# A segment softmax that divides by a second exponential, shares read from PSUM, node rows loaded in an earlier stage, and record scatters moved between stages

## The reference

```python
q, k, v = (x @ W + b).reshape(n, H, C)            # H = 4 heads, C = 32, for each of q, k, v
e  = (edge_attr @ We).reshape(-1, H, C)
kj, vj = k[src] + e, v[src] + e
alpha = einsum('ehc,ehc->eh', q[dst], kj) / sqrt(C)
amax  = segment_max(alpha, dst)
ex    = exp(alpha - amax[dst])
denom = segment_sum(ex, dst)
alpha = ex / (denom[dst] + 1e-16)                 # a softmax over the edges of one destination
agg   = segment_sum(vj * alpha[:, :, None], dst)
out   = agg.reshape(n, HID) + (x @ Wskip + bskip)  # then a two-layer gelu MLP on out
```

## Time and profile before

| what | us |
|---|---|
| median of 3 runs | 5401.89 (5398.77 to 5412.19) |
| span of the profiled execution | 4651.0 |
| softmax stage | 2062 to 2195 |
| weighing stage | 2197 to 2399 |
| stage of m1 and l2 | 2401 to 2568 |

### The profile page before, as it was taken

One profiled execution on the slowest core, in us unless ns is written; L12 is line 12 of the kernel. 1 busy time (PEld: TensorE's weight loads), 2 busy tenths in 40 slices (PEclk: granted clock), 3 DMA queues, 4 the chain that ended last, 5 costly groups with the idle time before them and its releaser, 6 DMA issues. The chain is left out here.

```text
span 4651.0 us, 50018 instructions
## 1 busy us (share of the span) xinstructions
PE 2871.3 (62%) x13750; PEld 2210.0 (48%) x13751; DVE 2230.8 (48%) x2711; ACT 613.9 (13%) x1076; POOL 3414.1 (73%) x3213
## 2 busy tenths in 40 slices
PE   3799998967777777751989643444444333333333
PEld 1688887943333333331989433333333333333333
DVE  7899997656666666668971621111111111111112
ACT  0355554010000000001751000000000000000000
POOL 1888886857777777767867677777777777777775
PEclk8899999968877878875999866666666566555556
DMA  6466566816666666651989523222222122212221
GB/s 191 139 189 183 170 187 209 265 37 172 170 170 170 170 171 173 173 153 59 278 241 276 174 68 94 68 68 68 68 68 68 49 53 52 53 53 53 53 53 51
DMA packets 498663, 599.91 MB, mean 129 GB/s; under 512 B 190115, under 2 KB 367441, under 8 KB 496248
## 3 DMA queue, kind: packets, MB, share of 16 engines
q0 software_dynamic: 117856, 246.12, 19.4%
q1 hardware_dynamic: 337751, 229.77, 17.7%
q10 hardware_dynamic: 42944, 122.68, 7.3%
HBM read 406.69 MB, written 204.36 MB: 131 GB/s over the span
## 5 line engine op out<-in xcount | busy, mean ns | idle before, releaser
L1151 PE MATMUL ps<-got,g_hot 128*128 x3224 | 719.2, 414 | 1151.3 <-DMA got<-y_back,s_msg 597.5
L721 POOL DMA_INDIRECT rec_by_src<-rec,pos x782 | 1123.9, 1437 | 344.1 <-issue 245.8
L1151 PEld LDWEIGHTS ps<-got,g_hot 128*128 128x128 f32 x3224 | 667.8, 316 | 1213.1 <-issue 1213.1
L1612 POOL DMA_INDIRECT sc_kv<-kv,d_src x806 | 762.0, 945 | 254.9 <-issue 245.3
L1036 POOL DMA_INDIRECT got<-y_forward,d_msg x782 | 739.1, 945 | 238.2 <-issue 238.2
L1036 POOL DMA_INDIRECT got<-y_back,s_msg x766 | 722.7, 943 | 241.7 <-issue 233.1
L806 PE MATMUL ps<-ln_low,ln_hot 128*125 128x256 f32 x2848 | 618.9, 380 | 19.7 <-DVE ln_low L783 15.9
L806 PEld LDWEIGHTS ps<-ln_low,ln_hot 128*125 128x125 f32 x2848 | 535.3, 188 | 103.2 <-issue 22.7
L1059 DVE TENSOR_TENSOR g_hot<-ps,src_loc 128x1024 f32<-128x1024 f32 x101 | 123.4, 1224 | 832.1 <-PE ps L1151 831.7
L1715 PE MATMUL ps<-q,sc_hotT 128*128 x1616 | 274.2, 322 | 236.4 <-DVE sc_hotT L1657 207.4
L1067 DVE TENSOR_TENSOR g_y<-ps,ms_b 128x384 f32<-128x384 f32 x75 | 41.8, 558 | 732.1 <-PE ps L1164 732.1
(11 more groups left out here) (328 smaller groups left out, 3102.4 us busy)
## 6 DMA issues: line engine op xcount, KB each, us to landing
linked<-ln_out SPq DMA_DIRECT2D x320, 224.0 KB
ve<-sc_kve ACTq DMA_DIRECT2D x202, 256.0 KB
wv_ve<-ve SPq DMA_DIRECT2D x101, 512.0 KB, 5.0
l_links<-linked SPq DMA_DIRECT2D x25, 800.0 KB, 7.3
l_links<-linked ACTq DMA_DIRECT2D x25, 800.0 KB, 9.2
attr_pairs<-ln_feats POOLq DMA_DIRECT2D x7, 2048.0 KB
sc_attr<-attr_pairs SPq DMA_DIRECT2D x202, 64.0 KB, 2.6
sc_kv<-kv,d_src POOLq DMA_INDIRECT x806, 3.0
```

What stands on the lines that cost most here:

```text
L721: pool.indirect_dma_start(out=dram["rec_by_src"], out_offset=bass.IndirectOffsetOnAxis(ap=S["pos"][:, c:c + 1], axis=0), in_=S["rec"][:, c ...
L1151: last = pe.matmul(ps[:, bass.ds(columns[j], width)], hot[:, q, j, :], got[:, bass.ds(slots[j], width)], start=False, stop=True, skip_grou ...
L1612: pool.indirect_dma_start(out=kv[:, q, j, :], out_offset=None, in_=dram["kv"], in_offset=bass.IndirectOffsetOnAxis(ap=S["d_src"][:, c:c + ...
```

## The change

- **Softmax, division.** The share is computed as exp(score - ln(sum + 1e-16)). The first exponential writes to `mx_back`, so that `mx_score` keeps the score less the maximum. After the last `carry` of each head ACT takes the logarithm with a bias of 1e-16, DVE subtracts, ACT takes a second exponential into `mx_score`. The addition, the reciprocal and the multiply of DVE go.
- **Softmax, node rows.** The four tiles of node numbers and places live for the whole layer. SP loads them in `scores`, ahead of step 24. The first entry is written in `index`.
- **Weighing.** Before each round of six groups DVE copies the shares of the 48 tiles from `alpha_cols` into PSUM (`hand`, 17 times), and the multiply reads them there. `hand` waits for the last multiply of the round before, and the next group waits for the copy; `weighed[5]` starts one higher for that, and PE waits for one more of it.
- **Scatters.** `index` 6 to 16 (ten of them ahead of its gathers), `m0` 30 to 38, softmax 82 to 16, weighing 100 to 138, `l2` 76 to 86; the norm stage keeps 52.

```diff
-RECORD_PARTS = {"index": 6, "link": 302, "l0": 70, "m0": 30, "project": 22, "maxima": 82, "weigh": 100, "m1": 42, "l2": 76, "norm": 0}
+RECORD_PARTS = {"index": 16, "link": 302, "l0": 70, "m0": 38, "project": 22, "maxima": 16, "weigh": 138, "m1": 42, "l2": 86, "norm": 0}
...
+            if send is not None:
+                first, last = part_of(send)
+                send_some(pool, S, dram, first, last - LATER)
             for k, s in enumerate(stairs):
                 pool.wait_ge(tiled, k + 1)
...
+                if n == 4 * WAYS:
+                    for name, a in (("before", dram["node"][0:rows]), ("node", dram["node"][1:1 + rows]), ("after", dram["node"][2:2 + rows]),
+                                    ("place", dram["loc"].rearrange("b e -> (b e)")[0:rows])):
+                        sp.dma_start(S["mx_" + name][:, :], a.rearrange("(p c) -> p c", p=P)).then_inc(S["noded"], 16)
                 sp.wait_ge(turned[q], i + 1)
...
                 act.wait_ge(ready, h + 1)
-                act.activation(score[:, h, :], score[:, h, :], ACT.Exp).then_inc(exped, 1)
+                act.activation(back[:, h, :], score[:, h, :], ACT.Exp).then_inc(exped, 1)
+            for h in range(HEADS):
+                act.wait_ge(summed, h + 1)
+                act.activation(back[:, h, :], back[:, h, :], ACT.Ln, bias=guard[:, 0:1]).then_inc(logged, 1)
+            for h in range(HEADS):
+                act.wait_ge(weighted, h + 1)
+                act.activation(score[:, h, :], score[:, h, :], ACT.Exp).then_inc(shared, 1)
...
                 carry(h, open_a, back, ALU.add, ALU.max)
-                link(dve.tensor_scalar_add(back[:, h, :], back[:, h, :], 1e-16))
-                link(dve.reciprocal(back[:, h, :], back[:, h, :]))
-                dve.tensor_tensor(score[:, h, :], score[:, h, :], back[:, h, :], ALU.mult).then_inc(shared, 1)
-            dve.wait_ge(shared, HEADS)
+                dve.engine_nop().then_inc(summed, 1)
+            for h in range(HEADS):
+                dve.wait_ge(logged, h + 1)
+                dve.tensor_tensor(score[:, h, :], score[:, h, :], back[:, h, :], ALU.subtract).then_inc(weighted, 1)
...
+            def hand(i):
+                dve.wait_ge(weighed[WAYS - 1], i + 1)
+                dve.tensor_copy(share, S["alpha"][:, :, bass.ds(start_of(i, 0), WAYS * GROUP)]).then_inc(handed, 1)
+                dve.wait_ge(handed, i + 1)
...
-                dve.tensor_tensor(ve4, ve4, S["alpha"][:, :, cols].rearrange("p a k -> p k a")
+                dve.tensor_tensor(ve4, ve4, share[:, :, q * GROUP:(q + 1) * GROUP].rearrange("p a k -> p k a")
...
             with dve.Fori(0, WHOLE) as i:
+                hand(i)
                 for q in range(WAYS):
                     group(i, q)
+            hand(WHOLE)
...
-                pe.wait_ge(weighed[q], i + 1)
+                pe.wait_ge(weighed[q], i + 1 + (q == WAYS - 1))
```

More of the change, by code:

```diff
@@ L439, in index_stage @@
         below = m.sb(tag + "_below", [P, TILES])
+        front = m.sb(tag + "_front", [1, 1])
+        fronted, begun = m.sem(tag + "_fronted"), m.sem(tag + "_begun")
+        LATER = 6
         ready, spread, tiled, stepped, flipped, listed = (m.sem(tag + n) for n in (
@@ L471, in _ @@
             if send is not None:
-                send_records(pool, S, dram, send)
+                send_some(pool, S, dram, last - LATER, last)
         @block.sync
         def _(sp):
+            sp.wait_ge(fronted, 1)
+            sp.dma_start(dram["node"][0:1].rearrange("(a n) -> a n", a=1), front[:, :]).then_inc(begun, 16)
             for k, s in enumerate(stairs):
@@ L488, in _ @@
             sp.wait_ge(filed, 16 * len(stairs))
+            sp.wait_ge(begun, 16)
             if sent:
@@ L533, in climb_of @@
                 dve.engine_nop().then_inc(stepped, 1)
+            dve.memset(front[:, :], -1.0).then_inc(fronted, 1)
             dve.wait_ge(spread, 1)
@@ L1616, in _ @@
         def _(sp):
+            rows = P * PAIRS_PAD
             for n in range(STEPS):
                 i, q = divmod(n, WAYS)
+                if n == 4 * WAYS:
+                    for name, a in (("before", dram["node"][0:rows]), ("node", dram["node"][1:1 + rows]), ("after", dram["node"][2:2 + rows]),
+                                    ("place", dram["loc"].rearrange("b e -> (b e)")[0:rows])):
+                        sp.dma_start(S["mx_" + name][:, :], a.rearrange("(p c) -> p c", p=P)).then_inc(S["noded"], 16)
                 sp.wait_ge(turned[q], i + 1)
@@ L1744, in softmax_maxima @@
         turn = m.sb("mx_turn", [P, HR, P])
[L1745 to L1748, removed]
+        node, node_b, node_a, loc = (S["mx_" + name] for name in ("node", "before", "after", "place"))
         bad = m.sb("mx_bad", [P, L])
@@ L1759, in softmax_maxima @@
         into = m.sb("mx_into", [P, HEADS])
-        front = m.sb("mx_front", [1, 1])
         turned, kept, stored, loaded, order, asked, told, ready, exped, shared, done = (m.sem("mx_" + n) for n in (
             "turned", "kept", "stored", "loaded", "order", "asked", "told", "ready", "exped", "shared", "done"))
-        fronted, noded = m.sem("mx_fronted"), m.sem("mx_noded")
+        summed, logged, weighted = (m.sem("mx_" + n) for n in ("summed", "logged", "weighted"))
+        guard = m.sb("mx_guard", [P, 1])
         divided, refilled = ([m.sem(f"mx_{n}{h}") for h in range(HEADS)] for n in ("divided", "refilled"))
@@ L1814, in _ @@
         def _(sp):
[L1815 to L1820, removed]
             for h in range(HEADS):
@@ L1838, in _ @@
             link = Chain(dve, order)
-            dve.memset(front[:, :], -1.0).then_inc(fronted, 1)
-            dve.wait_ge(noded, 16 * 4)
+            dve.wait_ge(S["noded"], 16 * 4)
+            link(dve.memset(guard[:, :], 1e-16))
             link(dve.tensor_scalar(bad[:, :], loc[:, :], 0.0, None, ALU.is_lt))
@@ L1901, in _ @@
             dve.wait_ge(exped, HEADS)
-            carried(2, False, same, score, top, 0.0, ALU.mult, ALU.add)
+            carried(2, False, same, back, top, 0.0, ALU.mult, ALU.add)
             for h in range(HEADS):
@@ L1931, in weigh_values @@
         iota = ps[:, 7 * BANK:7 * BANK + P]
+        share = ps[:, 7 * BANK + P:7 * BANK + P + HEADS * WAYS * GROUP].rearrange("p (a c) -> p a c", a=HEADS)
+        handed = m.sem("wv_handed")
         block = stack.enter_context(nc.Block())
@@ L2286, in gnn_kernel @@
             S["alpha"] = a.sb("alpha_cols", [P, HEADS, PAIR_COLS])
+            for name in ("before", "node", "after", "place"):
+                S["mx_" + name] = a.sb("mx_" + name, [P, PAIRS_PAD])
+            S["noded"] = a.sem("mx_noded")
             with ExitStack() as early:
```

6 lines of the change are left out of this document (3 added, 3 removed).

## The result

The changed kernel took 5591.35 us (median of 4 runs, 5580.35 to 5592.67) against 5401.58 before: a ratio of 1.0336, 95% interval 1.0318 to 1.0354. The forecast was 5393, with a range from 5378 to 5408. It is 190 us slower where 9 us less were forecast.

The account below looks back on a forecast made before the run. Stages end at barriers, so each touched stage was judged by who arrives last: DVE in weighing and at softmax's end, POOL nearly last in m1 and l2. -5.4 - 21.0 + 10.2 + 7 = -9.2 gave 5393 us, range 5378 to 5408.

Parts of the forecast that it names:

- The 750.9 outside of it, which I take as unchanged: Whole run: 750.9 us of the 5401.89 lie outside the profiled span of 4651.0 and stay the same.
- Weighing, multiply and scatters: 0: Weighing: multiply costs the same from PSUM, frees POOL; 138 scatters take 175 us under cover of DVE's 195; 0 us.
- The rival that ended on the slower side: Weighing: POOL stays held at one scatter a group, 1.86 us; stage +42, time 5425; chance 0.07.
- Stage of m1 and l2: +7: m1 and l2: ten more scatters at 1.27 make POOL end last, +7 us (0 to +8).
- m0: 0: m0: eight more scatters, 10.5 us, fit into POOL's idle 15.12; no cost.
- up to +5: Scores: four more loads on SP taken as 0, up to +5 us if they hold up one step.
- Softmax, start: -5.4: Softmax start: without the node loads the score loads start sooner, -5.4 us (-4.5 to -8.1).
- End: -21.0: Softmax end: logarithm, subtraction and second exponential replace addition, reciprocal and multiply, -21.0 us (-18.7 to -21.7).
- Copies: +10.2: Weighing: 17 copies with their waits enter DVE's chain, 0.67 us each, +10.2 us (+4.0 to +21.9).

Follow-up runs that it names:

- e1: The kernel before, unchanged, run and profiled again: 5406.47 us, ratio 0.9995.
- e3: The kernel before with only the shares copied into PSUM and read there, 100 scatters in weighing: 5544.7 us, ratio 1.0244.
- e5: The kernel before with the new softmax alone, node rows loaded in scores, first entry written in index, all scatters as before: 5405.65 us, ratio 0.9999.
- e8: The kernel before with the shares in PSUM and POOL waiting for one more DVE multiply ahead of each of weighing's 100 scatters: 5411.73 us, ratio 1.0012.
- e9: The kernel before with a useless POOL write of 200 numbers after each scatter in m0, project, m1 with l2, and norm: 5227.71 us, ratio 0.9648.
- e10: The kernel before with a useless POOL write of 24 numbers after each scatter in m0, project, m1 with l2, and norm: 5384.49 us, ratio 0.9931.
- e13: The changed kernel with a useless POOL write of 200 numbers after each scatter in m0, project, weighing, m1 with l2, and norm: 5371.85 us, ratio 0.9905.
- e7: The kernel before with ten useless two-operand DVE additions behind each of the 7 chunks of m1 with l2: 5401.98 us, ratio 1.0002.

## Why the prediction was wrong

**The time outside the span.** "The 750.9 outside of it, which I take as unchanged" is the step that failed first. These 751 us were inside the stages of the timed runs: e1 has 5398.4 of span beside 5400.12 of time, so the runs do not take 751 us more than their span. Every price was then read from an execution in which PE ran beside scatters 1.27 apart, as in `m1` with `l2` of the earlier trace rows. Why that one execution had no stops is not settled.

**Weighing, multiply and scatters: 0.** This is the term that failed, and the step in it is the overlap: 138 scatters of 175 us were taken to go out under cover of DVE's 195. They measured 176, and DVE's and PE's work came behind them in 206; the stage grew by 180, of which some ten are the copies. The rest of the mechanism was right as far as it went: the multiply costs the same from PSUM (1.22) and no longer holds POOL (0.96 throughout). The rival that ended on the slower side had POOL still held. What happened is the opposite: with POOL freed the stage lost 130 in e3 with 100 scatters, and 180 with 138, the copies' ten in each. The clause "no longer holds POOL" was booked as a gain of cover, without a rival in which POOL's pace falls on the others. One number spoke for such a rival: a time 16% above the span.

**Stage of m1 and l2: +7.** It was +13, 10 scatters at 1.27 each, since PE hardly works while they last. POOL was not last there, as the prediction had it: it was through 154.02 us before it began in the next stage, and the pause of 9.85 in the earlier trace rows came as one of 2.97. **m0: 0** was +16 with eight scatters more, which make 10 at 1.27; the other 6 are not explained. Scores grew by 4, inside the "up to +5" that was allowed.

**Softmax, start: -5.4.** This was right. The first work on the scores comes 19.4 after the stage's start (2384.5), where it came 24.2 after it in the earlier trace rows (2062.1): 4.8. **End: -21.0.** This was right as well. DVE and ACT of the changed kernel:

```profile
2403.93 4.13 DVE L1873 SCALAR_TENSOR_TENSOR mx_score<-mx_bad,mx_score 128x816 f32<-128x816 f32 x4 [4.91 <-DMA mx_score<-alpha]
...
2469.57 4.39 DVE L1896 SCALAR_TENSOR_TENSOR mx_back<-mx_openafter,mx_into,mx_back 128x816 f32<-128x816 f32 x4
```

```profile
2443.67 1.28 ACT L1820 ACT_TABLE_LOAD   x1
2470.73 4.30 ACT L1820 ACTIVATE mx_back<-mx_back,mx_guard 128x816 f32<-128x816 f32 x4 [25.78 <-DVEq L1921]
2475.04 1.28 ACT L1823 ACT_TABLE_LOAD   x1
2476.34 3.20 ACT L1823 ACTIVATE mx_score<-mx_score 128x816 f32<-128x816 f32 x4
2485.38 5.75 ACT L1827 ACTIVATE alpha_cols<-ps 128x128 f32<-128x128 f32 x28 [5.84 <-PE ps L1803]
```

From the first of the last carries (2469.57) to the end of the last exponential (2479.54) it is 10.0, against the 10.2 worked out; to the end of ACT's copies 21.6, against 42.6 before. Loads of 1.28 stand ahead of the logarithms and of the second exponential, where the Trainium skill (ScalarE: Activation LUTs, section "Table sets: the hidden batching unit") would have one load serve both; only the second of the two is on the path. The condition of this gain was missing: e5 shows that with 82 scatters the stage would not have become shorter at all.

**Copies: +10.2.** The sum was right, its parts less so: weighing in e8 is 10.5 longer than in e1, so one of the 17 costs 10.5 / 17 = 0.62. The copy itself took 0.36, above the 0.28 assumed and just outside the 0.35 that it was given at most; the gaps were smaller, and the two errors cancel.

## What to carry to other kernels

When a run's time is far above its profile's span, the profile may be of another kind of execution, as here, and no price read from it holds until a second profile of the same kernel has been taken. In this kernel a filler of indirect DMAs on POOL was free only with room between them; ask of every edit that frees POOL what its faster pace does to the others. Where PE shows "issue" in front of each matmul while POOL issues back to back, a useless pause on POOL is the cheapest test, and here it was worth 190 us (e9). An engine that idles long beside them need not be slowed itself: look first at what its buffer waits for.

## What the runs showed of the hardware

With 1.27 us from one scatter to the next (128 records each, issued by POOL), PE issued a matmul mostly every 2.8 us in e1, e3 and the changed kernel. At 1.34 the stage of `m1` and `l2` still took 294 (e10). At 1.48 it took 220 (e13 222), and at 1.49, 1.55 and 1.61 it took 183, 188 and 212, each within 8 of POOL's own time (118, 118 and 128 scatters); weighing was still slowed at 1.48 and free at 1.61 and 1.87. So the limit lies near 1.49 in these kernels. That 0.01 parts the two sides rests on different kernels, and the pace was not varied so finely in one.

The slowing sets in 12 to 19 us after the first scatter of a stage (e3, the changed kernel, e1) and outlasts the last by 6 to 12 us (e1). It is shown for PE's issue alone. DVE, ACT and SP idle long beside it, but in weighing they wait for PE's count, and of the 69 us between SP's two loads in e1 (2797.84 and 2866.51) the profile puts 68.3 down to waiting for PE. At that time DVE ran 15 operations between 2839.23 and 2843.11 with one gap of 0.27. One hole is not explained so: in e1 nobody but POOL begins anything that the trace counts between 2730.64 and 2797.84.

What the scatters and PE's issue share is not shown. DMA engines were 20% busy in e1's slowed stretch, and POOL kept its 0.97 and its gap of 0.30 but for one wait of 2.97. Nor is it shown why the first profile was free of it at the same 1.27.

The Trainium skill (SBUF — State Buffer, section "Who interferes with whom") has a DVE operation with two SBUF inputs contend with GpSimd's reads. The multiply of weighing agrees (1.56 for a scatter beside it against 0.97), the additions of e7 don't (0.97); the measurement decides, and two SBUF inputs alone are not enough to hold POOL's scatters.
